# A decoder of thirteen stages: three pairs of neighbouring stages put into one program block each

## The chip, the cores and the metric

One core of a Trainium2 chip runs the whole program. The metric is the time of one execution on the device, in microseconds (us). The engines are called PE (TensorE; PEld is its weight load), DVE (VectorE), ACT (ScalarE), POOL (GpSimd) and SP (SyncE, which here only issues DMAs). A suffix q, as in PEq or SPq, means the engine's sequencer and not its datapath.

## The reference

The program is four decoder layers of three sublayers each on x of 32 sequences of 64 tokens with 128 features, all in float32. Every sublayer is added to the residual and works on a normalised copy of it:

```python
x = x + _L0_attn_ref(_layernorm(x), ...)      # L0a
x = x + _L0_xattn_ref(_layernorm(x), ctx, ...) # L0x
x = x + _L0_ffn_ref(_layernorm(x), ...)       # L0f: 8 experts, each token goes to 2
x = x + _L1_attn_ref(_layernorm(x), ...)      # L1a: rotary attention, 16 heads of 64
x = x + _L1_xattn_ref(_layernorm(x), ctx, ...) # L1x
x = x + _L1_ffn_ref(_layernorm(x), ...)       # L1f: 8 experts, each token goes to 1
x = x + _L2_attn_ref(_layernorm(x), ...)      # L2a: queries and keys by low-rank maps, then normed per head
x = x + _L2_xattn_ref(_layernorm(x), ctx, ...) # L2x: gated matrix memory
x = x + _L2_ffn_ref(_layernorm(x), ...)       # L2f: 8 gated experts, each token goes to 2
x = x + _L3_attn_ref(_layernorm(x), ...)      # L3a: scores times a factor of distance
...                                           # L3x, L3f
```

A routed expert layer (L0f, L1f, L2f) chooses experts per token, sends the token's row to a slot of its expert, runs the expert on blocks of 256 slots, and adds the returned row, times its weight, to the token's residual.

## The kernel before

The 2048 tokens lie in 16 **tiles** of 128 tokens (one token in a partition), and four tiles are a **quarter**. The residual `x`, its normalised copy `h` and the work buffers `hn` and `att` (128 partitions x 16 tiles x 128) stay in SBUF. `arena` is scratch of 11 "rooms" of 1024 numbers a partition, `ps` is all of PSUM.

Each stage is a function that fills one `nc.Block()`: a list of instructions for each engine, in the order written. When a block is entered or left all engines drain and meet at a barrier. Within a block the only order between engines is that of semaphores. The stages take their semaphores in turn from two halves of 68 (`c.turn_over()`), and POOL clears the other half at a block's start (`c.begin(g)`, line 274).

The end of a routed expert layer (`routed_experts`) runs so. POOL scatters the last blocks' rows to `home_L0f` in DRAM (L1688). SP waits for them and loads the rows of all tokens back, a quarter at a time (`y_back`, L1536); in the kernel before they land in the first rooms of `arena`. DVE then goes through the quarters: it adds the rows to `x` (L1881), measures mean and variance (`measure`, L362 and L365), POOL makes the reciprocal deviation (`invert`, L372 and L374), and DVE writes `h` (`scale`, L381), one quarter behind:

```python
for q in range(QUARTERS):
    v.wait_ge(back[q], 16 * top)
    ...                                        # add the rows of the quarter, L1881
    measure(v, following, c.x, q, HT)
    if q > 0:
        scale(v, following, c.x, c.h, q - 1, HT)
scale(v, following, c.x, c.h, QUARTERS - 1, HT)
```

`scale` counts every tile that it has written in the semaphore `following.normed`. Nobody waits for that count; the next stage relies on the barrier.

The attention stage behind begins with PE turning `h`: four transposes for each quarter into PSUM, which ACT copies to `hT`.

- **L1a** (`rotary_attention`) turns all 16 tiles first (L1929; ACT copies, L2032), and PE then waits until all four quarters are copied (`pe.wait_ge(s.turned, QUARTERS)`). Behind that come tile 0's values (L1952, four matmuls in the trace) and its queries and keys (L1941, 16 matmuls each), then DVE rotates the queries as soon as they are there (L2094).
- **L2a** (`attention`, mode "latent") turns quarter 0 (L498, ACT L629). For each tile of it PE makes maps and values (L529, L512), ACT copies and squares them (L673 to L679), and DVE sums the squares (L774). When all four tiles are summed, DVE makes the norms (from L779), and PE turns the results, from which the first scores come.
- **L3a** (`attention`, mode "decay") turns quarter 0, makes keys and queries (L505, L506), ACT copies them (L639, L653), POOL spreads the keys of a tile over heads (`spread_keys`, L757), PE makes the scores (L554) and DVE takes them (L820).

In L1a SP also issues, at the start, three loads of the experts of L1f and the blanking of `slots_L1f` and `home_L1f` in DRAM (L299, L290, L293).

Of the kernel before, what the change touches and what calls it, by code (L numbers as in the profile page):

```python
# [37 lines left out]
SIGNALS = 68  # L38
# [169 lines left out]

class Turns:
# [4 lines left out]
class Core:  # L214


    def __init__(self, nc, ctx, where, big):
# [3 lines left out]
        self.halves = [[ctx.enter_context(nc.semaphore(f"signal_{h}_{i}")) for i in range(SIGNALS)]  # L221
# [6 lines left out]
        self.nt, self.own_tiles = NT, slice(0, NT)  # L228

# [99 lines left out]
NORM = "stats moments square var_eps rstd scaled weighted ready "  # L329
# [109 lines left out]
def attention(c, n, keys_from="h", mode="plain", q_scale=1.0, exp_scale=1.0, bias=False,  # L439
# [5 lines left out]
    c.turn_over()  # L445
    s = signals(c, "turned_ps turned q_ps k_ps v_ps q_ready keys_ready vx_ready kx_ready scores_ps factored scored "
                "max_ready shifted probs_ready probsT_ps probsT_ready o_ps inv_ready att_ready oT_ps "
                "oT_ready y_ps y_added bias_scaled")
    if rms:
        r = signals(c, NORM)  # L450
    else:
        following = unit_norm(c, 1)
# [4 lines left out]
    src = c.hn if rms else c.h  # L457

# [25 lines left out]
    with nc.Block() as block:  # L484
        if blanks:
            @block.sync
            def _(sp):
                c.blank_slots(sp, blanks)

        @block.tensor  # L490
        def _(pe):
            def turn(q):
                if rms:
                    pe.wait_ge(r.ready, HT * (q + 1))
                if q > 0:
                    pe.wait_ge(s.q_ready, HT * q)
                for t in tiles_of(q):
                    last = pe.transpose(c.ps[:, 6, tok(t % HT)], src[:, t], c.w("ident"))  # L498
                last.then_inc(s.turned_ps, 1)

            def keys_and_queries(q):
                pe.wait_ge(s.turned, q + 1)
                if q > 0:
                    pe.wait_ge(s.vx_ready, values_taken(q))
                pe.matmul(c.ps[:, 7], c.w(n + "_wk"), kvT[:, quarter(q)], start=True, stop=True).then_inc(s.k_ps, 1)  # L505
                pe.matmul(c.ps[:, 6], c.w(n + "_wq"), c.hT[:, quarter(q)], start=True, stop=True).then_inc(s.q_ps, 1)  # L506

            def values_of(t):
                wv = c.v_of_h[:] if latent else c.w(n + "_wv")
                for b in range(2):  # L510
                    for u in range(2):
                        last = pe.matmul(values_ps(t, u, b), kvT[:, seq(t, b)], wv[:, part(u)], start=True, stop=True)  # L512
                return last

            def values(q):
                pe.wait_ge(s.keys_ready, HT * (q + 1))
                for t in tiles_of(q):
                    last = values_of(t)
                last.then_inc(s.v_ps, 1)

            def latent_maps(t):

                pe.wait_ge(s.turned, t // HT + 1)
                if t >= 2:
                    pe.wait_ge(s.vx_ready, 2 * (t - 1))
                    pe.wait_ge(l.copied, t - 1)
                if t % HT == 1 and t > 1:
                    pe.wait_ge(s.keys_ready, t - 1)
                pe.matmul(maps_ps(t), c.hT[:, tok(t)], c.q_of_h[:], start=True, stop=True)  # L529
                values_of(t).then_inc(l.maps_ps, 1)  # L530

            def latent_turn(q):

                pe.wait_ge(l.copied, HT * (q + 1))
                pe.wait_ge(s.vx_ready, values_taken(q + 1))
                pe.wait_ge(l.q_normed, HT * (q + 1))
                for t in tiles_of(q):
                    last = pe.transpose(c.ps[:, 6, tok(t % HT)], c.att[:, t], c.w("ident"))
# [6 lines left out]
            def scores(t):  # L545
                pe.wait_ge(s.q_ready, t + 1)
                pe.wait_ge(s.kx_ready, t + 1)
                if t > 0:

                    pe.wait_ge(scores_read, t)  # L550
# [2233 lines left out]
```

## Time and profile before

| what | value |
|---|---|
| three runs | 1708.34, 1715.52, 1720.39 us; median 1715.52 us |
| the profiled execution | 1705.7 us, of which the span of the trace is 1703.9 us |
| PE busy | 1175.2 us, 69% of the span |
| DVE busy | 1064.7 us, 62% |
| POOL busy | 667.4 us, 39% |
| ACT busy | 627.9 us, 37% |
| granted TensorE clock, mean | 0.792 of full speed |
| DMA, mean over the span | 52 GB/s |

No engine is busy throughout: the stages follow each other, each with its own limit, and at each seam the engines stand while the next stage fills. The shares say little about a change at a seam; the timeline there does. The granted clock has two levels, 0.5 (1.2 GHz) and 1 (2.4 GHz); a value between them is a mean over a stretch that holds both.

### The profile page before, as it was taken

The page shows a single profiled execution, that of the slowest core. Times are in us where ns is not written, and L with a number is a line of the kernel's source. Part 1 is how long each engine was busy: PE and PEld are TensorE (multiplying, and loading weights), DVE is VectorE, ACT ScalarE, POOL GpSimd, SP SyncE. Part 2 cuts the span into 40 slices and gives each one's busy share as a digit, 9 for nine tenths or more (in the row PEclk, how much of TensorE's full clock was granted, in tenths as well). Part 3 has the DMA queues.
Part 4 walks back from the last instruction along what each step waited for, and adds up shares of the span by engine and source line. Part 5 has one row for each costly group of instructions (what it writes and reads, how often), then busy time and mean ns, then how long its engine had stood idle before and what let it go on. Part 6 is the DMA issues. An engine that isn't in the chain of part 4 may idle for free. (4 is left out here: it accounts for less than half of the span.)

```text
span 1703.9 us, 35618 instructions
## 1 busy us (share of the span) xinstructions
PE 1175.2 (69%) x14040; PEld 891.6 (52%) x14040; DVE 1064.7 (62%) x2853; ACT 627.9 (37%) x1475; POOL 667.4 (39%) x726
## 2 busy tenths in 40 slices
PE   7982438927888769654566853199938884776778
PEld 5652337816767646543244643178815551563556
DVE  4989601156899938833666598333449947856672
ACT  2641213305666646211544331012205433543343
POOL 3447444433555535443123224723333424324320
PEclk9985569968999979767677765599969856877878
DMA  8900136540000058021000100245410000000000
GB/s 269 141 2 2 42 113 177 162 137 2 3 3 3 3 85 119 3 82 64 0 1 1 26 1 1 101 134 170 158 50 1 2 1 1 1 2 1 1 2 26
DMA packets 72010, 89.13 MB, mean 52 GB/s; under 512 B 5823, under 2 KB 59138, under 8 KB 71200
## 3 DMA queue, kind: packets, MB, share of 16 engines
q1 hardware_dynamic: 65824, 76.89, 17.9%
q0 software_dynamic: 6016, 9.93, 1.7%
q8 instruction: 112, 1.84, 0.5%
q14 instruction: 58, 0.48, 0.1%
HBM read 56.55 MB, written 32.69 MB: 52 GB/s over the span
## 5 line engine op out<-in xcount | busy, mean ns | idle before, releaser
L757 POOL TENSOR_TENSOR arena<-arena,small 128x1024 f32<-128x1024 f32 x80 | 154.0, 1930 | 132.6 <-ACT arena L639 87.4
L372 POOL TENSOR_SCALAR var_eps<-moments 128x1 f32<-128x1 f32 (+1 forms) x136 | 37.1, 273 | 335.9 <-DVE moments L365 335.8
L687 ACT ACTIVATE arena<-arena 128x1024 f32<-128x1024 f32 x80 | 84.6, 1058 | 132.2 <-DVE arena L831 132.2
L554 PE MATMUL ps<-arena,q 64*64 64x512 f32 x640 | 102.6, 715 | 37.5 <-issue 20.6
L2079 POOL TENSOR_TENSOR arena<-arena 128x512 f32<-128x512 f32 x64 | 79.9, 1282 | 103.5 <-DVE arena L2097 103.5
L564 PEld LDWEIGHTS ps<-small,arena 128*128 128x128 f32 x640 | 80.7, 157 | 71.4 <-issue 37.2
L564 PE MATMUL ps<-small,arena 128*128 128x128 f32 x640 | 99.3, 305 | 12.3 <-ACT arena L687 10.6
L1598 PEld LDWEIGHTS ps<-expert_ring,arena 128*128 128x128 f32 (+1 forms) x864 | 104.5, 192 | 2.9
L712 ACT COPY arena<-ps 128x512 f32<-128x512 f32 x160 | 87.1, 588 | 50.4 <-PE ps L564 49.7
L1598 PE MATMUL ps<-expert_ring,arena 128*128 128x128 f32 (+1 forms) x864 | 104.7, 275 | 0.0
L374 POOL TENSOR_TENSOR rstd<-var_eps,minus_half 128x1 f32<-128x1 f32 (+1 forms) x136 | 99.8, 734 | 11.3
L576 PE MATMUL ps<-vx,arena 128*64 128x18 f32 x2560 | 98.1, 221 | 0.3 <-DVE x L845 0.3
L576 PEld LDWEIGHTS ps<-vx,arena 128*64 128x64 f32 x2560 | 90.0, 150 | 15.3 <-issue 11.9
L2025 ACT ACTIVATE arena<-arena,row_inv 128x64 f32<-128x64 f32 x256 | 85.8, 340 | 10.2 <-DVE row_inv L2112 10.1
L1579 PE MATMUL ps<-arena,expert_ring 128*112 128x256 f32 x368 | 85.1, 385 | 1.0 <-DMA expert_ring<-L2f_in 0.9
L1688 POOL DMA_INDIRECT home_L2f<-arena,home x46 | 44.7, 971 | 93.1 <-DVE arena L1839 68.7
L831 DVE TENSOR_TENSOR arena<-arena,row_max 128x1024 f32<-128x1024 f32 x64 | 78.8, 1231 | 2.2
L829 DVE TENSOR_REDUCE row_max<-arena 128x16 f32<-128x1024 f32 x64 | 78.1, 1220 | 2.2
L1566 PE MATMUL ps<-small,arena 128*128 128x128 f32 x108 | 22.3, 294 | 78.3 <-DMA arena<-slots_L2f 33.2
L824 DVE TENSOR_TENSOR arena<-ps,small 128x1024 f32<-128x1024 f32 x32 | 39.1, 1221 | 58.4 <-PE ps L554 58.4
L1644 ACT ACTIVATE arena<-ps 112x512 f32<-112x512 f32 x46 | 27.5, 597 | 126.8 <-PE ps L1579 126.8
L1579 PEld LDWEIGHTS ps<-arena,expert_ring 128*112 128x112 f32 x368 | 64.7, 180 | 14.8 <-DMA expert_ring<-L2f_in 1.1
(359 smaller groups left out, 2922.6 us busy)
## 6 DMA issues: line engine op xcount, KB each, us to landing
expert_ring<-L2f_in SPq DMA_DIRECT2D x23, 704.0 KB, 4.2
expert_ring<-L0f_in SPq DMA_DIRECT2D x23, 578.0 KB, 3.9
slots_L0f<-blank SPq DMA_DIRECT2D x1, 8385.0 KB, 50.0
slots_L2f<-blank SPq DMA_DIRECT2D x1, 8385.0 KB, 50.3
small<-small_in SPq DMA_DIRECT2D x1, 4231.5 KB, 19.0
expert_ring<-L1f_in SPq DMA_DIRECT2D x8, 512.0 KB, 3.9
arena<-slots_L0f SPq DMA_DIRECT2D x23, 129.0 KB, 3.1
arena<-slots_L2f SPq DMA_DIRECT2D x23, 129.0 KB, 3.5
```

The lines of the kernel that those rows point to most:

```text
L374: g.tensor_tensor(m.rstd_of[:, own], m.var_eps_of[:, own], c.minus_half[:, 0:n], ALU.pow).then_inc(m.rstd, 1)
L554: last = pe.matmul(c.ps[part(b), m], c.q[part(m), at:at + S], kx(t)[part(m), b * 512:(b + 1) * 512], start=True, stop=True)
L564: last = pe.transpose(c.ps[:, 2 + k, j * P:(j + 1) * P], buf(t)[:, (4 * k + j) * P:(4 * k + j + 1) * P], c.w("ident"))
L576: last = pe.matmul(o_ps(t)[part(b), j * 18:(j + 1) * 18], probsT(t)[:, seq(j, b)], c.vx[:, t % 8, b, j], start=True, stop=True)
L687: act.activation(buf(k), buf(k), ACT.Exp, scale=exp_scale).then_inc(s.probs_ready, 1)
L712: act.copy(probsT(t)[:, j * 512:(j + 1) * 512], c.ps[:, 2 + j])\
L757: g.tensor_tensor(kx(t).rearrange("p (b h k) -> p b h k", b=2, k=S), bcast(of_tile, 2, HEADS // 2), bcast(bcast(c.w("head_of_row"), 2, S), ...
L831: v.tensor_tensor(shaped, values, bcast(c.row_max[:, t], 2, S), ALU.subtract).then_inc(s.shifted, 1)
L1579: last = pe.matmul(c.ps[0:width, 2 * (m % 2) + k, cols], ring(j)[:, k * hid + i * width:k * hid + (i + 1) * width], xT(j), start=True, sto ...
L1598: last = pe.matmul(c.ps[:, 4 + j % 2, tok(b)], hidden(j)[:, i, tok(b)], ring(j)[0:width, down_at + i * D:down_at + (i + 1) * D], start=(i ...
L2025: last = act.activation(probs(t)[:, g * S:(g + 1) * S], probs(t)[:, g * S:(g + 1) * S], ACT.Exp, bias=c.row_inv[:, t, g:g + 1], scale=WH * ...
L2079: g.tensor_tensor(own_half, own_half, sines[i][:, (1 - half) * 512:(2 - half) * 512], ALU.add)\
```

## The change

Stages are gathered into groups, and one block is opened for a group and not for a stage: L0f with L1a, L1f with L2a, and L2f with L3a share a block; all others have their own. A stage function now adds its instructions to the open block `c.block`. Since no barrier stands between the two stages of a group, the turning of a quarter waits until its four tiles are counted in `normed`; and since the second stage may write `arena` while returned rows are still being added, these land in `att` and `hn`. POOL's clearing of semaphores moves into a small function of its own at each group's start, behind which POOL branches to the stage. L3f's two halves, which were two blocks before, stay so. The halves of semaphores have 90 and 47 members. In the diff, lines that are only indented otherwise are left out.

```diff
-SIGNALS = 68
+SIGNALS = (90, 47)
...
+def wait_tiles(engine, h_ready, count):
+    if h_ready is not None:
+        engine.wait_ge(h_ready, count)
...
 def attention(...):
-    c.turn_over()
...
+    h_ready = c.h_ready
...
-    with nc.Block() as block:
+    block = c.block
...
             def turn(q):
                 if rms:
                     pe.wait_ge(r.ready, HT * (q + 1))
+                else:
+                    wait_tiles(pe, h_ready, HT * (q + 1))
...
         @block.gpsimd
         def _(g):
-            c.begin(g)
...
 def routed_experts(...):
     following = unit_norm(c, 1)
+    c.h_ready = following.normed
...
-    y_back = c.room(0, 2 * top).rearrange("p (k t d) -> p k t d", k=top, t=NT)
+    y_back = (c.att, c.hn)
...
-                    sp.dma_start(y_back[:, k, own(q)], home[:, own(q)]).then_inc(back[q], 16)
+                    sp.dma_start(y_back[k][:, own(q)], home[:, own(q)]).then_inc(back[q], 16)
...
 def rotary_attention(c):
...
             for q in range(QUARTERS):
+                wait_tiles(pe, h_ready, HT * (q + 1))
                 for t in tiles_of(q):
                     last = pe.transpose(c.ps[:, q, tok(t % HT)], c.h[:, t], c.w("ident"))
...
+GROUPS = (("L0a",), ("L0x",), ("L0f", "L1a"), ("L1x",), ("L1f", "L2a"), ("L2x",), ("L2f", "L3a"), ("L3x",), ("L3f",),
+          ("L3m",))
+
+def run_together(c, group):
+    c.turn_over()
+    c.h_ready = None
+    with c.nc.Block() as c.block:
+        @c.block.gpsimd
+        def _(g):
+            c.begin(g)
+        for n in group:
+            STAGES[n](c)
...
-        for n in stages:
-            STAGES[n](c)
+        for group in groups:
+            run_together(c, group)
```

Three places in the engines' queues show it. Line numbers of the kernel after are a few higher than those of the kernel before.

PE from the last matmuls of L0f into L1a, before: the branch waits for the barrier, the 16 transposes wait for nothing, and the values wait for `turned` (signal_1_1).

```order
L1598 MATMUL ps<-expert_ring,arena 128x128 [waits signal_0_42,signal_0_40]
L1598 MATMUL ps<-expert_ring,arena 128x128 x7
L1491 UNCONDITIONAL_BRANCH
L1925 UNCONDITIONAL_BRANCH [waits barrier_Pool_Activation_PE_DVE_SP_release]
L1929 MATMUL ps<-small,h 128x128 x16
L1952 MATMUL ps<-L_qkv,hT 128x512 [waits loaded_L1_qkv,signal_1_1]
```

The same place after; signal_0_48 is `normed` of L0f, signal_0_50 is `turned`, and the first two of the four quarters' pairs are shown.

```order
L1604 MATMUL ps<-expert_ring,arena 128x128 [waits signal_0_32,signal_0_30]
L1604 MATMUL ps<-expert_ring,arena 128x128 x7
L1930 UNCONDITIONAL_BRANCH
L1935 MATMUL ps<-small,h 128x128 [waits signal_0_48]
L1935 MATMUL ps<-small,h 128x128 x3
```

The order of the work is the same; each quarter's first transpose has a wait of its own in the barrier's place.

PE at the start of L2a, before:

```order
L1491 UNCONDITIONAL_BRANCH
L490 UNCONDITIONAL_BRANCH [waits barrier_Pool_Activation_PE_DVE_SP_release]
L498 MATMUL ps<-small,h 128x128 x4
L529 MATMUL ps<-q_of_h,hT 128x384 [waits signal_0_1]
L512 MATMUL ps<-v_of_h,hT 64x64 x4
```

PE at the start of L2a, after; signal_0_51 is `normed` of L1f, signal_0_53 is `turned`.

```order
L498 UNCONDITIONAL_BRANCH
L508 MATMUL ps<-small,h 128x128 [waits signal_0_51]
L508 MATMUL ps<-small,h 128x128 x3
L539 MATMUL ps<-q_of_h,hT 128x384 [waits signal_0_53]
L522 MATMUL ps<-v_of_h,hT 64x64 x4
```

PE, which stood at the barrier until all four quarters were normalised, now stands there until the first one is.

POOL from the end of L2f into L3a, before: the last of four `invert`, the barrier, the clearing (ISA), and the keys' spreading, which waits for `keys_ready`.

```order
L372 TENSOR_SCALAR var_eps<-moments 128x4 [waits signal_0_57]
L374 TENSOR_TENSOR rstd<-var_eps,minus_half 128x4 [waits signal_0_58]
L1491 UNCONDITIONAL_BRANCH
L740 UNCONDITIONAL_BRANCH [waits barrier_Pool_Activation_PE_DVE_SP_gather]
L274 ISA
L757 TENSOR_TENSOR arena<-arena,small 128x1024 [waits signal_1_6] x2
```

The same place after; signal_0_62 is `keys_ready` of L3a.

```order
L380 TENSOR_SCALAR var_eps<-moments 128x4 [waits signal_0_53]
L382 TENSOR_TENSOR rstd<-var_eps,minus_half 128x4 [waits signal_0_54]
L750 UNCONDITIONAL_BRANCH
L766 TENSOR_TENSOR arena<-arena,small 128x1024 [waits signal_0_62] x2
```

The first spreading still stands behind all four `invert` of L2f in POOL's queue, with one branch between them.

## Rows read from the trace of the kernel before

**Rows 1.** The page: the span of the profiled execution.

```profile
span 1703.9 us, 35618 instructions
```

**Rows 2.** Groups of instructions by line: PE's turning of `h` in `attention`.

```profile
L498 PE MATMUL ps<-small,h 128*128 128x128 f32 x64 | 13.9, 355 | 56.3 <-PEq L1491 50.3 <-PEq L1914 5.0 <-PEq L2636 0.9
```

**Rows 3.** Timeline at L0f's end and L1a's start: start, length, engine, what [idle <-releaser].

```profile
350.11 2.19 DVE L1881 SCALAR_TENSOR_TENSOR x<-arena,tiny,x 128x128 f32<-128x128 f32 x8 [8.89 <-DMA arena<-home_L0f]
...
356.67 1.08 DVE L381 TENSOR_SCALAR h<-x,moments,rstd 128x128 f32<-128x128 f32 x4
...
361.95 2.18 DVE L1881 SCALAR_TENSOR_TENSOR x<-arena,tiny,x 128x128 f32<-128x128 f32 x8
...
366.79 1.12 DVE L381 TENSOR_SCALAR h<-x,moments,rstd 128x128 f32<-128x128 f32 x4 [0.47 <-POOL rstd L374]
368.18 2.83 SPq L299 DMA_DIRECT2D expert_ring<-L1f_in  x3
...
368.22 3.30 PE L1929 MATMUL ps<-small,h 128*128 128x128 f32 x16 [27.46 <-PEq L1491]
369.35 0.59 ACT L2032 COPY hT<-ps 128x512 f32<-128x512 f32 x1 [31.28 <-PE ps L1929]
...
372.20 1.98 PE L1952 MATMUL ps<-L_qkv,hT 128*128 128x512 f32 x4 [0.68 <-ACT hT L2032]
...
376.01 1.22 DVE L2094 TENSOR_TENSOR arena<-ps,small 128x1024 f32<-128x1024 f32 x1 [8.10 <-PE ps L1941]
```

**Rows 4.** Busy time by stretch; the granted clock is the third number from the right.

```profile
368.20:372.00 3.80, 3.30 (x16) 3.09 (x16) 0.00 (x0) 2.12 (x4) 0.00 (x0) 0.63 0.76 255
372.00:376.00 4.00, 3.80 (x22) 2.84 (x23) 0.00 (x0) 1.16 (x2) 0.00 (x0) 1.00 1.08 308
811.00:813.00 2.00, 2.00 (x19) 0.93 (x18) 0.42 (x1) 1.37 (x5) 0.00 (x0) 0.91 0.00 0
1278.00:1280.00 2.00, 2.00 (x17) 0.95 (x14) 1.97 (x2) 1.69 (x3) 0.39 (x1) 0.75 0.00 0
```

**Rows 5.** Timeline at L1f's end and L2a's start.

```profile
794.14 1.08 DVE L381 TENSOR_SCALAR h<-x,moments,rstd 128x128 f32<-128x128 f32 x4
...
802.16 1.12 DVE L381 TENSOR_SCALAR h<-x,moments,rstd 128x128 f32<-128x128 f32 x4 [0.48 <-POOL rstd L374]
...
803.60 1.08 PE L498 MATMUL ps<-small,h 128*128 128x128 f32 x4 [22.39 <-PEq L1491]
...
809.09 0.42 DVE L774 TENSOR_REDUCE tiny<-arena 128x32 f32<-128x256 f32 x1 [5.81 <-ACT arena L679]
...
814.66 0.42 DVE L774 TENSOR_REDUCE tiny<-arena 128x32 f32<-128x256 f32 x1 [0.98 <-ACT arena L679]
```

**Rows 6.** Timeline at L2f's end and L3a's start.

```profile
1256.13 1.08 DVE L381 TENSOR_SCALAR h<-x,moments,rstd 128x128 f32<-128x128 f32 x4
...
1265.18 1.04 POOL L374 TENSOR_TENSOR rstd<-var_eps,minus_half 128x4 f32<-128x4 f32 x1
...
1267.68 1.09 PE L498 MATMUL ps<-small,h 128*128 128x128 f32 x4 [27.90 <-PEq L1491]
...
1272.27 3.77 POOL L757 TENSOR_TENSOR arena<-arena,small 128x1024 f32<-128x1024 f32 x2 [6.06 <-ACT arena L639]
...
1274.32 1.98 PE L554 MATMUL ps<-arena,q 64*64 64x512 f32 x8 [1.10 <-POOL arena L757]
...
1280.39 2.75 POOL L757 TENSOR_TENSOR arena<-arena,small 128x1024 f32<-128x1024 f32 x1 [2.00 <-PE ps L554]
```

**Rows 7.** Timeline at the start of L0x, behind its barrier.

```profile
128.66 2.37 DVE L1400 TENSOR_TENSOR arena<-h,small 128x512 f32<-128x512 f32 x2 [0.32 <-PEq L484]
129.06 1.41 POOL L1384 TENSOR_TENSOR arena<-hn,small 128x512 f32<-128x512 f32 x1 [1.11 <-SPq L1321]
```

**Rows 8.** The page's DMA issues: KB each, median us from issue to landing.

```profile
arena<-home_L0f SPq DMA_DIRECT2D x8, 256.0 KB, 4.8
...
home_L1f<-blank SPq DMA_DIRECT2D x1, 1024.0 KB, 11.8
```

More of the change, by code:

```diff
@@ new lines, in _ @@
+                    act.activation(c.oT[:, tok(t)], oT_ps(t), ACT.Identity, bias=c.w(n + "_bv"))\
+                        .then_inc(s.oT_ready, 1)
+                else:
+                    act.copy(c.oT[:, tok(t)], oT_ps(t)).then_inc(s.oT_ready, 1)
+            if k < nt:
+                weights(k)
+            if ahead < quarters:
+                if latent and step < 2:
+                    for t in range(HT * ahead + 2 * step, HT * ahead + 2 * step + 2):
+                        take_maps(t)
+                if latent and step == 2:
+                    take_roots(ahead)
+                if latent and step == 3:
+                    take_queries(ahead)
+                    take_keys(ahead)
+                if not latent and step == 1:
+                    take_keys(ahead)
+                    take_queries(ahead)
+                if not latent and step == 2:
+                    take_values(ahead)
@@ new lines, in _, with take_values @@
+    @block.scalar
+    def _(act):
+        def take_values(q):
+            for i, n in enumerate(SETS):
+                act.activation(vT(i)[:, quarter(q)], c.ctxT[:, quarter(q)], ACT.Identity,
+                               bias=c.w("L0x_bv" + n), scale=c.w("L0x_wv" + n)).then_inc(s.v_ready, 1)
+        take_values(0)
+        take_values(1)
+        for q in range(QUARTERS):
+            act.wait_ge(s.shifted, q + 1)
+            act.activation(score(q), score(q), ACT.Exp, scale=D ** -0.5).then_inc(s.exp_ready, 1)
+            if q + 2 < QUARTERS:
+                take_values(q + 2)
@@ new lines, in _ @@
+        for q in range(QUARTERS):
+            turn(q)
+            logits(q)
+            if q > 0:
+                rank(q - 1)
+        rank(QUARTERS - 1)
+        if not capped:
+            pe.wait_ge(s.logits_ready, 1)
+            pe.matmul(c.ps[:, 4, 0:E], c.w("ones"), upto[:, NT], start=True, stop=True).then_inc(s.total_ps, 1)
+        pe.wait_ge(s.logits_ready, QUARTERS)
+        turn_slots(0)
+        turn_slots(1)
+        up(0)
+        for j in range(BLOCKS):
+            if j + 2 < BLOCKS:
+                turn_slots(j + 2)
+            if j + 1 < BLOCKS:
+                up(j + 1)
+            down(j)
@@ L1900, in rotary_attention @@
     w = c.big["L1_qkv"]
+    h_ready = c.h_ready
     CH = INNER // P
```

3396 lines of the change are left out of this document (1668 added, 1728 removed).

## The prediction, on record before the kernel ran

> **What bounds the kernel now.** The change touches three seams, so I read those and not the shares of the span. First the groups by line: PE's turning of `h` in `attention` stood 56.3 us before it began, 50.3 of them behind the end of L1f and L2f [rows 2]. That is a sum of idle time of PE, not of time that can be won: DVE is busy nearly throughout, adding returned rows and normalising. So next the timeline, seam by seam, to see what the last normalised tile is followed by.
>
> At L0f's end the last `scale` begins at 366.79 and lasts 1.12, and PE's first transpose comes at 368.22 [rows 3]. So the barrier itself costs 0.31 us there (368.22 less 367.91), and 0.32 and about as much at the others [rows 5, 6]. What costs is behind it: the next stage's filling. In L1a it is 16 transposes and four copies before the values at 372.20 [rows 3]. In L2a it runs from the transposes at 803.60 to the last of quarter 0's sums at 814.66, during which DVE has next to nothing to do [rows 5]. In L3a it runs from 1267.68 to the first scores at 1274.32 [rows 6]. Quarter 0, which these fillings need, is normalised long before: its `scale` ends at 357.75, at 795.22 (794.14 plus 1.08) and at 1257.21 (1256.13 plus 1.08) [rows 3, 5, 6]. The change lets the fill begin there.
>
> DVE's own tail, four quarters from 350.11 to 367.91 at L0f's end [rows 3], stays: it comes in the same order with the same operands, read from `att` and `hn` and not from `arena`. I cost the new place of the returned rows at nothing: same sizes, same queue, and no instruction more.
>
> **L2a, the largest term.** PE's transposes begin when quarter 0 is counted, 795.22 plus the 0.07 or so from a count to its waiter: 795.29, which is 8.3 us before 803.60. Behind them come PE, ACT and PE again, none of which has other work at L1f's end. So the sums, which end ACT's chain, become possible 8.3 us earlier: the first at 800.8 for 809.09, the fourth at 806.36 for 814.66. Is DVE free? It ends its last `scale` at 803.28 (802.16 plus 1.12) [rows 5], so it comes late to the first sum or two, does them at 0.42 each, and waits for the fourth as before. The fourth one carries the norms and everything behind. Gain: **8.3 us**. The clock moves it: it rose within 811 to 813, at about 811.4 by the mean of 0.91 [rows 4], when three of four tiles were through PE. A rise a tile or so earlier or later in the chain is worth, as an estimate, 1 us either way (three steps of the sums took 5.57 us, 1.9 each, and half a step is lost or won for each tile). So 7.3 to 9.3.
>
> **L3a.** PE and ACT can make keys and queries of quarter 0 long before L2f's end (1257.28 plus the 4.6 from 1267.68 to 1272.27 is 1261.9 for the keys). But POOL, which spreads them, has its four `invert` ahead in the queue, and the last of them ends at 1266.22 (1265.18 plus 1.04) [rows 6]. So the wait for keys is replaced by POOL's own order: the first spreading begins at 1266.27 and not at 1272.27, which is 6.0 us earlier, and scores and DVE follow it as before (PE at 1268.3 for 1274.32; DVE is free from 1267.36 on). Two costs stand against it. The first spreading lies beside DVE's last `scale` for 1.1 us, which it didn't before. A spreading takes 1.9 (two in 3.77), and one took 2.75 [rows 6]: 0.0 to 0.9 lost. `scale` reads one tensor, and POOL's `invert` took 1.04 beside it in these tails, so I take a small part, 0.3. And POOL takes a branch in between. Gain: **5.6 us**, of 4.9 to 6.0.
>
> **L1a.** PE waits for all quarters here, so only three quarters' turning is taken off the path. The last `scale` ends at 367.91; PE's four transposes begin at 367.98, ACT's copy begins 1.13 later (369.35 less 368.22) and takes 0.59, and the values begin at 369.75: 2.45 us before 372.20 [rows 3]. Against it stands the clock. The 16 transposes on end were what raised it: a mean of 0.63 over 368.2 to 372.0 puts the rise at about 371.0, and the values and queries then ran at the full clock [rows 4]. They took 3.81 us from 372.20 to DVE's first step at 376.01 [rows 3]. After the change PE comes to them from four-transpose bursts 4 us apart. If the clock is at half for all of it, the 3.7 us of matmuls in it (PE is busy 3.80 of 4.00 there [rows 4]) double and the seam loses 1.2; if it has risen before, the whole 2.45 is won. Where the clock rose in the other two fillings, whose work also comes in bursts, it took 7.8 us from the first transpose in L2a (811.4) and 11.3 in L3a (1279.0, by the mean of 0.75 in 1278 to 1280) [rows 4 to 6]. That is nearer to the cold end, so I take **0.6 us**, of -1.2 to 2.45. The Trainium skill (TensorE: Matmul & The Clock Gate, Part 1) says that the array's clock is at half when idle and rises only after sustained work. By that rule L1a's bursts don't raise it, its term is near -1.2 and the sum near 12.6; the rows above agree as far as they go.
>
> **POOL's branch.** Every group now has one branch more on POOL, behind the clearing. At L0x POOL is on the path at once: its first work began at 129.06, where DVE's began at 128.66 [rows 7]. So clearing and branching together cost at most 0.4 there, and one more branch is a small part of it; it matters at L0x and at L3a, where POOL leads, and elsewhere POOL waits for others first. I take 0.1 us in all, of 0 to 0.8. The Trainium skill (Runtime: NRT & Kernel Launch, Instruction fetch mechanics) warns that a taken branch can leave what the sequencer has fetched ahead and stall for a fetch; that speaks against this change. Taken at 0.4 for each place where POOL leads, the sum would be 0.8 less the 0.1, that is 0.7 us worse. The row shows no stall beyond these 0.4.
>
> **SP's transfers.** The three loads and the blanking of L1a, issued from 368.18 on, now follow the returned rows at once, at about 350. They are hidden: quarter 3's rows are first needed at 361.95 [rows 3], and a load of 256 KB lands 4.8 us after its issue [rows 8].
>
> **The sum.** 8.3 + 5.6 + 0.6 - 0.1 = 14.4 us. Against the profiled execution that is 1705.7 - 14.4 = 1691.3 (its span was 1703.9 [rows 1]; nothing outside the span changes). That execution was faster than each of the three runs shown, whose median is 1715.52, so I carry the difference to the median: 1715.5 - 14.4 = **1701 us**, 0.84% faster. The bounds of the terms give 10.2 (7.3 + 4.9 - 1.2 - 0.8) to 17.75 (9.3 + 6.0 + 2.45).
>
> A difference of 1%, here 17 us, is about what a measurement of this kernel can tell from no change; its three runs lie 12 us apart.
>
> **Rivals.**
>
> *Everything falls well.* The clock rises early in all three fillings: 17.75 us, 1697.8, which is past 1%. For it: nothing ties the time of the rise to the program's start of a stage, so it comes differently each time. Against it: three seams would have to be lucky at once. But the scatter of the runs helps it, and later stages, which begin some 14 us earlier, may get their rises earlier or later too. I give it 0.24.
>
> *The clock stays low and POOL is held up.* All terms at their bad ends: 10.2 us, 1705.3. For it: bursts with gaps in the rows of L2a and L3a. Against it: in L2a and L3a the fillings were at half clock before as well, so they have little to lose. 0.14.
>
> *The seam doesn't open.* If ACT or PE still stood until DVE's tail ended (a count that is passed late, or a step of the old stage still in the queue), only the barriers would go: three times 0.31, 1714.6. The rows of the queues speak against it: PE has only its branch and the wait for the first quarter ahead. 0.04.
>
> *The early transfers hold up the returned rows: slower.* At L0f's end SP's loads of experts and 2 MB of blanking now start while returned rows are still in flight. The blanking of `home_L1f` landed 11.8 us after its issue [rows 8], so the burst lasted from 368.2 to about 383, some 15 us. If it overtakes the rows, DVE stands at a quarter for them. Up to 14.4 us of it is paid by the other seams; from there on the kernel is slower. If quarter 1's rows, needed some 3 us behind quarter 0's at 350.11 [rows 3], came only behind the whole burst and their own 4.8 us (350.1 + 15 + 4.8 = 370), DVE would lose 17 us: 14.4 - 17 is 2.6 us slower, 1718. Against it: the rows are issued first on the same queue, and quarter 0 had landed by then. Past 1% slower it gets only with the scatter's help. 0.04.
>
> The rest, 0.54, is for the forecast, 1698.5 to 1704.
>
> **Chances and range.** Past 1% faster: the first rival's 0.24, and 0.06 of the forecast by scatter: 0.30. Within 1%: 0.66. Slower by over 1%: 0.04, the last rival and plain bad luck. The range adds the scatter of the runs, some 6 us either way of a median, to the terms' bounds and leaves the last two rivals out only in part: 1688 to 1712.
>
> **What would show it.** In the trace after: quarter 0's transposes of L2a some 0.1 us behind its `scale`, and the fourth sum 3 us behind DVE's last `scale`, not 11.4; POOL's first spreading in L3a within 0.1 us of its last `invert`, with ACT's copies of keys long done; L1a's values 1.8 us behind the last `scale`, and a granted clock there that is lower than before. DVE's tail should have its lengths unchanged. Wrong would be: a DVE that waits for DMA between quarters at L0f's end, a POOL whose first work in L0x comes over 0.5 us behind DVE's, or a PE whose transposes of quarter 0 still stand behind quarter 3.

## The result, and the profile after

The changed kernel took 1700.38 us, median of 13 runs (1691.16 to 1707.32), beside 1717.78 us, median of 13 runs of the kernel before (1707.48 to 1725.33). The ratio on record, which isn't that of the two medians (they lie 17.4 us apart), is 0.9919, with a 95% interval of 0.9894 to 0.9944: 13.9 us less (0.0081 times 1717.78), and by the interval 9.6 to 18.2. The profiled execution took 1700.2 us; its page says:

```profile
span 1698.3 us, 35588 instructions
```

The span is only 5.6 us shorter than before [rows 1], though the three seams gained more. The part ahead of the first seam was 10.2 us longer in this profile: DVE's first addition behind L0f came at 360.28, not at 350.11 [rows 3]. The opening of the seams isn't the cause: with all seams closed (a barrier between the two stages), the kernel rows_only (below) has it at 360.43, and in the profiles of all kernels but before and one whose edit lies there it is 355.3 to 367.9. Nor is the new place of the rows, which rows_only shares: timed against before, that kernel is by the interval at most 6.2 us slower (1.0036). The profiled execution of before lay 12.1 us under its median, so its profile was a lucky one, and the seams are read one by one.

**Seam A (L0f into L1a).** The timeline after, answering to [rows 3]:

```profile
360.21 1.95 SPq L306 DMA_DIRECT2D expert_ring<-L1f_in  x3
360.28 1.14 DVE L1886 SCALAR_TENSOR_TENSOR x<-att,tiny,x 128x128 f32<-128x128 f32 x4 [8.80 <-DMA hn<-home_L0f]
...
362.75 7.60 SPq L300 DMA_DIRECT2D home_L1f<-blank  x1
...
363.62 0.61 DVE L1886 SCALAR_TENSOR_TENSOR x<-att,tiny,x 128x128 f32<-128x128 f32 x2
...
368.05 1.12 PE L1935 MATMUL ps<-small,h 128*128 128x128 f32 x4 [17.03 <-DVE h L389]
...
377.03 1.11 DVE L389 TENSOR_SCALAR h<-x,moments,rstd 128x128 f32<-128x128 f32 x4 [0.48 <-POOL rstd L382]
...
378.20 1.11 PE L1935 MATMUL ps<-small,h 128*128 128x128 f32 x4 [0.47 <-DVE h L389]
...
379.99 3.78 PE L1958 MATMUL ps<-L_qkv,hT 128*128 128x512 f32 x4 [0.68 <-ACT hT L2038]
...
383.57 4.85 PE L1947 MATMUL ps<-hT,L_qkv 128*128 128x128 f32 x32
...
386.66 1.23 DVE L2099 TENSOR_TENSOR arena<-ps,small 128x1024 f32<-128x1024 f32 x1 [8.52 <-PE ps L1947]
```

PE now waits for DVE's `scale` by quarter and not for its own queue. The last `scale` ends at 378.14 (377.03 plus 1.11); the values begin 1.85 us behind it, as forecast, where it was 4.29 before. But four values took 3.78 us for 1.98 [rows 3], and DVE's first rotation comes 8.52 us behind the last `scale` for 8.10. The busy time by stretch tells why; the granted clock is the third number from the right, as in [rows 4]:

```profile
368.04:377.72 9.68, 3.34 (x12) 2.15 (x12) 9.14 (x43) 1.17 (x2) 2.94 (x5) 0.50 1.14 248
...
379.99:383.57 3.58, 3.58 (x5) 1.50 (x6) 0.00 (x0) 0.00 (x0) 0.00 (x0) 0.50 0.00 0
383.57:386.66 3.09, 3.09 (x19) 3.09 (x18) 0.00 (x0) 1.01 (x1) 0.00 (x0) 0.62 0.00 0
```

PE was busy 3.34 of 9.68 us while it turned by quarter, and all of the values ran at 1.2 GHz; in the profile of before, 16 transposes on end had brought it to 2.4 ahead of them [rows 4].

**Seam B (L1f into L2a).** The timeline after, answering to [rows 5]:

```profile
803.00 1.09 DVE L389 TENSOR_SCALAR h<-x,moments,rstd 128x128 f32<-128x128 f32 x4
...
804.14 1.12 PE L508 MATMUL ps<-small,h 128*128 128x128 f32 x4 [13.96 <-DVE h L389]
...
811.04 1.12 DVE L389 TENSOR_SCALAR h<-x,moments,rstd 128x128 f32<-128x128 f32 x4 [0.47 <-POOL rstd L382]
...
812.07 0.74 DVE L783 TENSOR_REDUCE tiny<-arena 128x32 f32<-128x256 f32 x2
...
814.09 0.42 DVE L783 TENSOR_REDUCE tiny<-arena 128x32 f32<-128x256 f32 x1 [1.28 <-ACT arena L689]
...
815.49 0.42 DVE L783 TENSOR_REDUCE tiny<-arena 128x32 f32<-128x256 f32 x1 [0.98 <-ACT arena L689]
```

PE's transposes come 0.05 us behind quarter 0's `scale` (804.09), and the fourth sum 3.33 us behind the last one (812.16), where it was 11.38.

**Seam C (L2f into L3a).** The timeline after, answering to [rows 6]:

```profile
1258.66 1.11 PE L508 MATMUL ps<-small,h 128*128 128x128 f32 x4 [17.57 <-DVE h L389]
...
1262.62 0.59 ACT L649 COPY arena<-ps 128x512 f32<-128x512 f32 x1 [2.22 <-PE ps L515]
...
1266.58 1.04 POOL L382 TENSOR_TENSOR rstd<-var_eps,minus_half 128x4 f32<-128x4 f32 x1
1267.59 3.77 POOL L766 TENSOR_TENSOR arena<-arena,small 128x1024 f32<-128x1024 f32 x2
1267.65 4.30 DVE L389 TENSOR_SCALAR h<-x,moments,rstd 128x128 f32<-128x128 f32 x4 [0.47 <-POOL rstd L382]
1269.64 1.99 PE L564 MATMUL ps<-arena,q 64*64 64x512 f32 x8 [5.41 <-POOL arena L766]
...
1271.87 1.22 DVE L829 TENSOR_TENSOR ps<-ps,decay 128x1024 f32<-128x1024 f32 x1
```

POOL's first spreading stands right behind its last `invert`, 6.1 us sooner than before. It wasn't stretched; DVE's last `scale` beside it was, 4.30 us for some 1.1. DVE's decay begins as soon as that is done, 0.24 us behind the scores (1269.64 plus 1.99 is 1271.63).

The table gives, from each profile, the time from DVE's first addition of a tail to its first step of the next stage (A: first rotation, B and C: first step on the scores). The upper three kernels have all seams closed or made to wait, the next three one or two open, the others all.

| kernel | A | B | C | sum |
|---|---|---|---|---|
| before | 25.89 | 38.16 | 27.35 | 91.40 |
| rows_only | 26.19 | 38.09 | 26.45 | 90.73 |
| late_turning | 27.77 | 37.83 | 25.65 | 91.25 |
| seam_L2a | 28.28 | 30.03 | 26.79 | 85.10 |
| seam_L3a | 26.24 | 38.32 | 21.17 | 85.73 |
| without_L1a | 26.17 | 29.15 | 20.90 | 76.22 |
| after | 26.39 | 30.12 | 20.90 | 77.41 |
| loads_first | 25.65 | 28.93 | 20.89 | 75.47 |
| spread_early | 24.88 | 29.30 | 21.55 | 75.73 |
| spread_wait | 26.23 | 30.68 | 22.33 | 79.24 |
| warm | 24.84 | 27.85 | 21.41 | 74.10 |
| warm_same | 24.03 | 27.09 | 20.90 | 72.02 |
| warm_more | 22.99 | 27.86 | 20.90 | 71.75 |
| warm_L1a | 22.99 | 29.22 | 21.57 | 73.78 |

### The profile page after: what moved, and what is told of

The parts are those of the page before. It is cut to its first block and busy times, and to the rows that moved or that the text cites. A ratio compares the mean times of both kernels' runs of the same rounds, so it can differ in the third digit from the quotient of the medians.

```text
span 1698.3 us, 35588 instructions
## 1 busy us (share of the span) xinstructions
PE 1179.8 (69%) x14040; PEld 895.6 (53%) x14040; DVE 1068.3 (63%) x2853; ACT 628.5 (37%) x1475; POOL 667.5 (39%) x726
## 3 DMA queue, kind: packets, MB, share of 16 engines
q8 instruction: 112, 1.84, 0.5%
## 5 line engine op out<-in xcount | busy, mean ns | idle before, releaser
L2031 ACT ACTIVATE arena<-arena,row_inv 128x64 f32<-128x64 f32 x256 | 85.8, 340 | 10.2 <-DVE row_inv L2117 10.1
L1693 POOL DMA_INDIRECT home_L2f<-arena,home x46 | 44.7, 972 | 95.7 <-DVE arena L1844 69.0
L1693 POOL DMA_INDIRECT home_L0f<-arena,home x46 | 44.7, 972 | 70.7 <-DVE arena L1842 46.4
```

The source lines that it names most:

```text
L1693: g.indirect_dma_start(home_dram[:, :], bass.IndirectOffsetOnAxis(ap=c.home[:, PER * j + k:PER * j + k + 1], axis=0), y(j)[:, k], None, bo ...
L2031: last = act.activation(probs(t)[:, g * S:(g + 1) * S], probs(t)[:, g * S:(g + 1) * S], ACT.Exp, bias=c.row_inv[:, t, g:g + 1], scale=WH * ...
```

## The experiments

**One seam at a time: seam_L2a, seam_L3a, without_L1a.** Only the groups change (and the sizes of the two halves of semaphores):

```diff
-GROUPS = (... ("L0f", "L1a"), ("L1x",), ("L1f", "L2a"), ("L2x",), ("L2f", "L3a"), ...)
+GROUPS = (... ("L0f",), ("L1a",), ("L1x",), ("L1f", "L2a"), ("L2x",), ("L2f",), ("L3a",), ...)      # seam_L2a
+GROUPS = (... ("L0f",), ("L1a",), ("L1x",), ("L1f",), ("L2a",), ("L2x",), ("L2f", "L3a"), ...)      # seam_L3a
+GROUPS = (... ("L0f",), ("L1a",), ("L1x",), ("L1f", "L2a"), ("L2x",), ("L2f", "L3a"), ...)          # without_L1a
```

> Only L1f and L2a share a block. Theory (the gain is the next stage's filling, begun behind quarter 0): the fourth of quarter 0's sums starts 3.3 us behind DVE's last scale and not 11.4, the first scores reach DVE 16.5 us behind it and not 24.6, so 8.05 us faster, a ratio of 0.9953; the seams into L1a and L3a read as before (8.1 us from the last scale to the first rotation; 10.15 us from POOL's last invert to DVE's first step). Rival (the gain is the barrier and its drains): 0.3 us, a ratio of 0.9998, with the fourth sum still 11 us behind.

> Only L2f and L3a share a block. Theory (filling begun early, bounded by POOL's queue): DVE's first step comes 4.3 us behind POOL's last invert and not 10.15, so 5.9 us faster, a ratio of 0.9966, with the other two seams as before. Rival (barrier alone): 0.3 us, 0.9998, DVE's first step 9.8 us behind.

> L1f with L2a and L2f with L3a share blocks; L0f and L1a have one each. Theory (the seam into L1a gains nothing, since PE reaches its values 2.4 us sooner and then runs them at the half clock): 13.95 us faster than before, a ratio of 0.9919, level with the changed kernel; DVE's first rotation 8.1 us behind the last scale. Rival (that seam is worth its 2.4 us of earlier values in most executions): 11.5 us, a ratio of 0.9933.

Ratios to the kernel before: seam_L2a 0.9948 (0.9914 to 0.9982), seam_L3a 0.9935 (0.9909 to 0.9961), without_L1a 0.9923 (0.9893 to 0.9953). B and C each carry a gain of their own, and without A the kernel is level with the changed one: A is worth nothing that can be measured (the two intervals are 4 and 5 us wide to either side). L3a alone gave more than expected: 11.2 us (0.0065 times 1719.58, the median before in that comparison), from 6.7 up by the interval, where its seam shows 5.7 (21.17 beside the mean 26.86 of before, rows_only and seam_L2a). What won the rest stays open; with both seams open it isn't there (13.2 us for without_L1a).

**The same blocks, but every turning waits for all tiles: late_turning.**

```diff
 def wait_tiles(engine, h_ready, count):
     if h_ready is not None:
-        engine.wait_ge(h_ready, count)
+        engine.wait_ge(h_ready, NT)
```

> The changed kernel with every turning waiting until all 16 tiles are normalised. Theory (the gain is the early filling): only the barriers go, 0.3 us at each of three seams: 0.9 us, a ratio of 0.9995; the fourth sum in L2a starts 11.1 us behind the last scale, DVE's first step in L3a 9.9 us behind the last invert, and in L1a the first rotation 7.8 us behind the last scale. Rival (the gain comes from fewer barriers, drains and branches wherever they stand): most of the gain stays, a ratio near 0.992.

It took 0.9975 (0.9946 to 1.0003), with the seams as long as closed ones (91.25 beside 91.40 and 90.73). So the barriers themselves are worth little (nothing by the seams, at most 9.3 us by the interval); the wait by quarter is the gain.

**The place of the returned rows alone: rows_only** (the kernel before with `y_back = (c.att, c.hn)`).

> The programs stay apart as before; only the returned rows get a place of their own. My theory (the whole gain lies in the three seams, the returned rows lie elsewhere only so that the seams can open): level with the kernel before, ratio 1.000, and the three seams as before: the values some 4.4 us, the fourth sum 11.4 us and the first spreading 6.06 us behind the last scale or invert. Rival (the place of the returned rows is worth something by itself, through its transfers): 0.997 or less. The profile also tells whether SP's slow walk in the first expert layer (0.7 to 1.4 us from one instruction to the next from 218 to 244 us in the changed kernel, 0.1 to 0.3 us in the one before) comes with this edit.

It took 1.001 (0.9984 to 1.0036), with seams as before: the place costs nothing and wins nothing.

**SP's transfers ahead of the returned rows: loads_first.** The three loads, the blanking and the code that issued them in L1a move:

```diff
+        if n == "L0f":
+            for e in range(SLOTS):
+                c.load_expert(sp, "L1f", e)
+            c.blank_slots(sp, "L1f")
         for q in range(QUARTERS):
```

> The changed kernel with SP's loads of the next expert layer and its blanking placed ahead of the returned rows of the first layer, not behind them. My theory (the early transfers cost nothing in the changed kernel because SP issues them behind the returned rows): the rows are now behind 30 MB-scale traffic on SP's own queue, VectorE's tail of additions starts 5 to 15 us later and the kernel is slower than the changed one by as much, ratio 0.995 to 1.001 against the kernel before. Rival (the queues have room for both, so the order is free): the tail starts where it does in the changed kernel, ratio 0.992.

The kernel took 0.9998 (0.9967 to 1.0029) and gave the whole gain back. The timeline of its SP and DVE:

```profile
358.52 1.29 SPq L306 DMA_DIRECT2D expert_ring<-L1f_in  x3
359.86 0.43 SPq L297 DMA_DIRECT2D slots_L1f<-blank  x1
360.33 5.43 SPq L300 DMA_DIRECT2D home_L1f<-blank  x1
365.81 5.86 SPq L1546 DMA_DIRECT2D att<-home_L0f  x1
...
376.53 1.14 DVE L1890 SCALAR_TENSOR_TENSOR x<-att,tiny,x 128x128 f32<-128x128 f32 x4 [23.01 <-DMA hn<-home_L0f]
```

DVE begins 18.0 us behind SP's first issue (376.53 less 358.52). In the changed kernel SP issues the first returned row at 356.51 and DVE begins 3.8 us later. So the burst costs 14.2 us if the rows stand behind it, and nothing when they stand ahead. (The expectation writes 30 MB for the transfers: they are 3.5 MB, three loads of 512 KB and 2 MB of blanks.)

**POOL and DVE at seam C: spread_wait and spread_early.** In the one POOL's first spreading waits for all 16 scaled tiles, in the other it is moved ahead of POOL's last `invert`:

```diff
+            if t == 0 and mode == "decay":
+                wait_tiles(g, h_ready, NT)                            # spread_wait
...
+            if k == 0 and mode == "decay":
+                invert(c, g, c.before_me, QUARTERS - 1, HT)           # spread_early, behind spread_keys(0)
...
-        for q in range(QUARTERS):
+        for q in range(QUARTERS - (n == "L2f")):                      # spread_early, in L2f
             invert(c, g, following, q, HT)
```

> The changed kernel, except that POOL's first spreading behind the third layer waits until VectorE has scaled all 16 tiles. My theory (VectorE's last scale took 4.30 us in place of 1.11 because POOL's spreading ran beside it, and this costs little, since the scores wait for the spreading anyway): the scale is back at 1.1 us, the spreading starts some 1.2 us later, and VectorE's first decay comes some 5.4 us behind the last invert, not 4.26: 1.2 us slower, which no timing here can tell, ratio 0.991 to 0.994. Rival (the stretch has another cause, such as TensorE's reads or the scale's own wait): the scale stays at 4 us, and the decay comes at 5.5 us or later.

> The changed kernel with POOL's first spreading behind the third layer placed ahead of its last invert, so that it waits for the first quarter alone. My theory (VectorE's decay waits for scores that wait for the spreading, which waits behind the last invert in POOL's queue: 4.26 us from invert to decay): the first spreading is over before the invert and the decay comes 1 to 3 us sooner against VectorE's last addition, ratio 0.991. Rival (POOL's 3.8 us spreading held the port beside VectorE's last scale, 4.30 us in place of 1.11; beside VectorE's additions it stretches those as much and delays the last invert itself): the tail from its start to the decay is as long as in the changed kernel (20.9 us) or longer, ratio 0.992 or more.

spread_wait took 0.9942 (0.9912 to 0.9971), spread_early 0.9929 (0.9905 to 0.9953), neither apart from the changed kernel. The timeline of spread_wait:

```profile
1272.80 1.11 DVE L389 TENSOR_SCALAR h<-x,moments,rstd 128x128 f32<-128x128 f32 x4 [0.47 <-POOL rstd L382]
1274.06 3.77 POOL L768 TENSOR_TENSOR arena<-arena,small 128x1024 f32<-128x1024 f32 x2 [1.29 <-DVE h L389]
...
1278.16 1.23 DVE L831 TENSOR_TENSOR ps<-ps,decay 128x1024 f32<-128x1024 f32 x1 [4.24 <-PE ps L564]
```

and of spread_early:

```profile
1273.46 3.45 POOL L766 TENSOR_TENSOR arena<-arena,small 128x1024 f32<-128x1024 f32 x1
1274.02 1.13 DVE L1889 SCALAR_TENSOR_TENSOR x<-hn,tiny,x 128x128 f32<-128x128 f32 x4
...
1277.19 1.04 POOL L382 TENSOR_TENSOR rstd<-var_eps,minus_half 128x4 f32<-128x4 f32 x1
...
1278.21 3.77 POOL L766 TENSOR_TENSOR arena<-arena,small 128x1024 f32<-128x1024 f32 x2
1278.27 4.30 DVE L389 TENSOR_SCALAR h<-x,moments,rstd 128x128 f32<-128x128 f32 x4 [0.50 <-POOL rstd L382]
```

With the spreading behind it, the `scale` is back at 1.11, and the decay comes 5.39 us behind the last `invert` for 4.26: the spreading is the cause, and running beside it still wins 1.1 us. Moved ahead, the spreading takes 3.45 beside DVE's additions, which keep their 1.13, and it holds back the last `invert`, whose first step comes 0.91 us behind the start of DVE's last moments (1276.89 and 1275.98) for 0.45 in the changed kernel (1266.26 and 1265.81). Then the next two spreadings stretch the `scale` just the same. Seam C is 21.55, which isn't the 1 to 3 us less that the first theory expected: that theory falls, and the rival's "as long" holds. "Longer" isn't shown, since kernels whose open seam C is untouched have 20.89 to 21.57.

**The clock in seam A: warm, warm_more, warm_L1a, warm_same.** Dummy multiplications that nobody reads fill TensorE's pauses; nothing else changes.

```diff
+def keep_busy(c, pe, n):
+    for _ in range(n):
+        pe.matmul(c.ps[:, 7, 0:256], c.w("ident"), c.ctxT[:, 0:256], start=True, stop=True)
...
+        if latent:                                       # L2a; not in warm_L1a
+            pe.wait_ge(c.h_measured, 1)                  # L1f's first statistics
+            keep_busy(c, pe, 5)
         turn(0)
...
             last.then_inc(s.turned_ps, 1)                # L1a, behind each turned quarter
+            keep_busy(c, pe, (3, 3, 0, 0)[q])            # warm_more, warm_L1a: (5, 5, 2, 1), and 6 ahead of quarter 0
+                                                         # warm_same: 512 + 256, 512 + 256, 256, 256 columns
```

> The changed kernel with dummy multiplications of 256 columns that nobody reads, put into TensorE's idle time in two seams: three each after the first two turned quarters ahead of the values (A), five ahead of the first turned quarter behind the second layer (B). My theory (in seam A the values and queries run at 1.2 GHz, 3.78 and 4.85 us a group, because TensorE idles between turned quarters, and that eats the 2.5 us by which they start sooner): the granted clock there rises towards 2.4 GHz, VectorE's first rotation comes 6.0 to 6.5 us behind the last scale, not 8.5, the fourth sum of B some 1 us sooner than 3.3, and the kernel takes 2 to 4 us less than the changed one, ratio 0.990. Rival (the seam is bound by the chain of turning, not by the clock, or the dummies themselves delay the turned quarters): rotation at 8.5 or later, ratio 0.992 to 0.994.

> The changed kernel with dummy multiplications of 256 columns that nobody reads: in seam A six ahead of the first turned quarter (from the first statistics on) and 5, 5, 2, 1 after the four, in seam B five ahead of the first quarter. The kernel warm (3, 3, 0, 0 in A) still had its values at a granted clock of 0.50, 3.62 us for four, and its queries at 1.00, 3.73. My theory (the clock is what holds seam A up): values in some 2.0 us, first rotation 5.0 to 5.4 us behind the last scale against 6.8 in warm and 8.5 in the changed kernel, seam B as in warm (first scores 14.3 us behind the last scale, 16.5 in the changed kernel), together some 5 us under the changed kernel: ratio 0.986 to 0.990. Rival (the dummies push back the turned quarters or the clock falls all the same): rotation at 7 us or later, ratio 0.990 to 0.992. If warm's 0.987 was more than its two seams give, this run comes back to 0.989.

> The same with the dummies of seam A alone; seam B is that of the changed kernel. My theory: seam A as in warm_more (rotation 5.0 to 5.4 us behind the last scale), seam B with its first scores 15.5 to 16.5 us behind the last scale, ratio 0.988 to 0.992, between the changed kernel and warm_more. Rival (the dummies in B carry it all): level with the changed kernel.

> As warm, with six dummies in seam A and five in seam B, and so with as many instructions ahead of the attention's tiles as warm has, but larger and otherwise spread: 512 and 256 columns behind the first turned quarter, the same behind the second, 256 behind the third and the fourth. In warm_more and warm_L1a, with 19 dummies, TensorE stood still for 1.1 to 1.9 us without waiting for anything seven and six times in the attention stage behind seam A, each time 193 or 194 instructions into a block of 256 of its program, and gave back what the seam had won; in warm and in the kernels without dummies there is no such hole in that stage. My theory (the holes come from where the instructions stand in TensorE's program): with the number of warm none in the attention stage, 412 to 415 us from the first rotation to the second tail as in warm, seam A's rotation 5.0 to 6.0 us behind the last scale, ratio 0.984 to 0.989. Rival (the holes and the lost time come with the warmer seam itself, whatever the count): holes of over 1 us in the attention stage, 424 us or more there, ratio 0.996.

warm took 0.9869 (0.9835 to 0.9903), warm_more 0.9975 (0.9942 to 1.0007), warm_L1a 0.9973 (0.9940 to 1.0007); the last two missed the ratios expected of them. warm's first rotation comes 6.82 us behind the last `scale`, a little over the 6.0 to 6.5 expected. In the seam the clock theory holds: warm_more's stretches, the turning and then the values and queries, read

```profile
366.50:377.26 10.76, 7.88 (x39) 5.86 (x37) 10.22 (x47) 1.76 (x3) 3.57 (x5) 0.97 1.11 240
378.70:382.45 3.75, 3.75 (x22) 2.79 (x23) 0.00 (x1) 1.01 (x1) 0.00 (x0) 1.00 0.00 0
```

and its first rotation comes 5.19 us behind the last `scale`, for 8.52; seam A is 22.99 for 26.39. Yet by its ratio the kernel is slower than the changed one. The stage behind, from the first rotation of L1a to the tail of L1f, took 424.6 us in warm_more and 426.0 in warm_L1a, for 411.9 in the changed kernel and 414.0 in warm. The timeline of warm_more's PE there, L1985 being the scores:

```profile
404.64 2.24 PE L1985 MATMUL ps<-arena 32*64 32x64 f32 x127 [5.77 <-POOL arena L2097]
407.94 0.36 PE L1985 MATMUL ps<-arena 32*64 32x64 f32 x1 [1.06 <-issue]
408.23 3.64 PE L1971 MATMUL ps<-L_qkv,hT 128*128 128x512 f32 x4
```

and of warm's:

```profile
402.03 2.25 PE L1983 MATMUL ps<-arena 32*64 32x64 f32 x128 [5.77 <-POOL arena L2095]
404.21 2.51 PE L1969 MATMUL ps<-L_qkv,hT 128*128 128x512 f32 x4
```

PE stands for 1.06 us between the 127th and 128th multiplication of one group, waiting for nothing ("issue"). All of TensorE's records in the trace (weight loads, multiplications, waits and drains) were counted from the program's start. Eight such holes, of over 1 us and up to 1.9 between weight loads, lie in warm_more's attention stage, in front of numbers 6849, 7361, 7874, 8385, 8898, 9409, 9922 and 10433. They make 11.7 us in all, beside the 12.7 by which the stage is longer than in the changed kernel, and each may lower the clock again: the values behind the first one took 3.64 us for 2.51. (The expectation of warm_same, below, counts seven; it lacks the one at 7361, of 1.84 us.) Divided by 256, each number leaves 193 or 194. In warm_L1a there are six, all at numbers of this list; in the kernels before and after, and in warm, none in that stage. A place in the tile doesn't explain them, since a tile has 511 records there and the holes stand 512 apart. Nor do the dummies or the warmer seam alone: all fourteen kernels have such holes in L0x, a stage that no edit touches, and the numbers there (3521 or 3522, 4033 or 4034) leave 193 or 194 too. Divided by 512 they leave 449 or 450, and those of warm_more 193 or 194, so the period is 256. The timeline of before's PE there:

```profile
154.17 0.84 PE L1334 MATMUL ps<-arena 64*32 64x32 f32 x58
156.02 0.96 PE L1334 MATMUL ps<-arena 64*32 64x32 f32 x70 [1.01 <-issue]
```

So TensorE's program comes in blocks of 256, and a hole can open at a block's edge. Most open where a block is run through fast: the edge before lies 3.4 to 3.9 us ahead of seven of warm_more's eight holes, and 3.1 and 3.5 us ahead of before's two, while in the same tiles of the changed kernel edges follow each other by 6.1 us or more, and in warm by 5.7 or more. That isn't the whole rule: two blocks of warm_L1a took 2.3 us with no such hole, and the edge before the hole at 6849 lies 9.3 us back, with a wait of 5.8 us for POOL between. The scores of one tile are 256 instructions (128 loads, 128 multiplications) in 1.6 to 2.3 us; 19 dummies instead of 6 moved the edges near both ends of them. The Trainium skill (Runtime: NRT & Kernel Launch, Instruction fetch mechanics) states that refills come in blocks of 256 instructions and that crossing one is mostly hidden: the trace agrees with the size, and shows what crossing costs where it isn't hidden.

warm_same put this to the test: as many instructions as warm, larger ones. It has no hole in that stage, took 415.4 us there, and 0.9847 (0.9813 to 0.9882), clear of the changed kernel's interval. Its seam A (24.03) is warmer than warm's and less warm than warm_more's, so against the rival, that the holes come with the warmth, the places of the holes say more than this run. Its timeline:

```profile
376.32 0.66 PE L1945 MATMUL ps<-small,h 128*128 128x128 f32 x4 [0.91 <-DVE h L395]
...
382.19 1.11 PE L1945 MATMUL ps<-small,h 128*128 128x128 f32 x4 [0.50 <-DVE h L395]
...
383.98 2.57 PE L1969 MATMUL ps<-L_qkv,hT 128*128 128x512 f32 x4
386.39 3.73 PE L1958 MATMUL ps<-hT,L_qkv 128*128 128x128 f32 x32
```

The clock still fell ahead of the last quarter (1.11 for 0.66), so its rotation comes 6.24 us behind the last `scale`, a little over the 5.0 to 6.0 expected. The three seams together are 5.4 us shorter than in the changed kernel (72.02 for 77.41); by the ratios the lead is larger, 12 us (0.9919 less 0.9847), and where the rest lies stays open: the two weren't timed side by side.

## Why the prediction was right, and where it was off

**The forecast** of 14.4 us, 1701, met 13.9 us and 1700.38. That the time was met so closely is in part luck: the base of 1715.5, a median of three, lay 2.3 us under the median of 13, and the two medians lie 3.0 us further apart than the forecast. The mechanism is what the seams show. By the table, closed seams against open ones (the four warm kernels left out; their untouched seams B and C would move no term by over 0.2), the terms are:

- **L2a, 8.3 (7.3 to 9.3).** Closed (before, rows_only, seam_L3a) 38.19 in the mean, open (after, seam_L2a, without_L1a, loads_first, spread_early, spread_wait) 29.70: 8.5. The chain went as worked out: transposes 0.05 us behind quarter 0's `scale`, two sums found DVE late, the third and the fourth were waited for, the fourth 3.33 behind the last one. The open ones lie between 28.93 and 30.68, about the width that was given for the clock, and the clock orders them: it rose 1.9 to 2.8 us ahead of the last `scale`'s end in the three shortest (28.93 to 29.30), 0.1 and 0.4 us behind it in the next two, and 2.0 us behind it in the longest.
- **L3a, 5.6 (4.9 to 6.0).** Closed 26.86, open (after, seam_L3a, without_L1a, loads_first) 20.97: 5.9. POOL's queue set the start, as forecast. The cost taken for the overlap, up to 0.9 on POOL, was laid on the wrong engine: DVE's `scale` paid it, and at most the last 0.24 us of that reached the path.
- **L1a, 0.6 (-1.2 to 2.45).** Closed (before, rows_only, seam_L2a, seam_L3a, without_L1a) 26.55, open (after, loads_first, spread_early, spread_wait) 25.79: 0.8, and in the profile after alone 0.5 the other way (26.39 for 25.89). The closed ones alone lie between 25.89 and 28.28, so the 0.8 can't be told from nothing, and that it came near 0.6 is luck. The clock ate the 2.45 us, as the cold end said: in all four open profiles the values took 3.4 to 3.8 us for 1.98. But the 16 transposes on end don't always raise it, as the prediction had it: in seam_L2a and late_turning, which have them on end too, the values took 3.78 and 3.74 us. warm_more, which keeps the clock up, has the seam at 22.99.
- **POOL's branch, 0.1 (0 to 0.8).** At L0x POOL's first work comes 0.54 us behind DVE's (134.98 and 134.44), for 0.41 before [rows 7]. That is just past the 0.5 us that the prediction named as a sign of being wrong, and the size, 0.13, is right for another reason. The clearing of semaphores, before and after, took (shortest, median and longest, in ns):

```profile
L274 POOLq EVENT_SEMAPHORE_RANGE_CLEAR  x15: 393/396/399, 28.2 to 1703.2; - x15
L281 POOLq EVENT_SEMAPHORE_RANGE_CLEAR  x12: 284/406/524, 28.5 to 1697.5; - x12
```

  The one at L0x is the longest, 524 for 396, since the changed kernel clears 90 semaphores there and not 68. In seam_L2a and without_L1a, which have the same branch and 49 to clear, POOL comes 0.32 us behind. So the branch costs nothing that is seen, and the prediction left out the larger half of semaphores.
- **SP's transfers, nothing.** Quarter 1's additions at 363.62 waited for no DMA. The cover that was named, the order on SP's queue, is the right one, and loads_first prices it at 14.2 us, near the 17 of the rival.

**The rivals.** That the seam doesn't open fell, and late_turning shows what would have been left. The group of PE's turning in `attention`, answering to [rows 2], now waits for DVE's `h` and hardly for PE's own queue:

```profile
L508 PE MATMUL ps<-small,h 128*128 128x128 f32 x64 | 14.0, 358 | 37.5 <-DVE h L389 31.5 <-PEq L2749 5.1 <-PEq L2637 0.9
```

That the transfers make the kernel slower fell for the reason given against it. Neither "everything falls well" nor "the clock stays low and POOL is held up" came whole. The clock was low in seam A; in B it rose ahead of the fourth tile's maps and in C behind the first scores, as before, so these had little to win or lose by it; and POOL's spreading kept its length.

## What to carry to other kernels

A barrier between two stages costs little by itself; what costs is the filling behind it, and a wait by quarter takes that off the path where the producer's tail is long and another engine leads the next stage. Where the matrix engine then gets its work in small bursts it may do it at half clock, so read the granted clock on both sides of the seam. And before filling a pause with dummy work, count instructions: 13 dummies more put block edges at both ends of a dense run of 256 small instructions, and this kernel lost by that more than the pause had held.

## What the runs showed of the hardware

DVE's `scale` and POOL's spreading exclude each other, and the one that starts second waits: one `scale` of a tile took at most 1943 ns beside the spreading and 340 otherwise, while the spreading kept its 1.9 us. The instructions of L389 in 1266 to 1273 us of the changed kernel, with their shortest, median and longest time:

```profile
L389 DVE TENSOR_SCALAR h<-x,moments,rstd x8: 312/340/1943, 1266.1 to 1271.6; 128x128 f32<-128x128 f32 x8
```

Where DVE's additions, with two tensors in, were already running, it was the spreading that took 3.45 us. The Trainium skill (SBUF — State Buffer, Who interferes with whom) says that the two engines share a pair of ports by an exclusive lock and that the one that issues second is blocked whole: the trace agrees, with 0.06 us between the two starts (1267.59 and 1267.65).

SP's instructions in L0f stood mostly 0.7 to 1.4 us apart, from 218.3 to 244.1 in the changed kernel, where in the kernel before the same ones followed each other within 0.5 us. rows_only, with its seams closed, shows the same from 223.3 to 243.5, so the opening of the seams doesn't bring it. All kernels but before have it, and all but before have the rows in their new place, so that isn't ruled out by the profiles; what brings it stays open.
